# Three re-placements in a step table of an attention and feed-forward kernel: pair 1's projections, the norm products of the steps without a tail, and the tail's second up products

## The reference

```python
q = einsum('bsd,hde->bhse', x, Wq); k, v alike
scores = where(causal, q @ k.T / sqrt(64), -inf)
out = softmax(scores) @ v
y = x + heads @ Wo;  y = layernorm(y, 1e-3) * gamma + beta
x1 = layernorm(x + y, 1e-5)
h = silu(x1 @ wg.T) * (x1 @ wu.T)          # int weights / 127
out = layernorm(x1 + h @ wd.T, 1e-5)
```

## Time and profile before

| what | value |
|---|---|
| median of 3 runs | 1460.8 us (1460.03 to 1463.27) |
| the profiled execution's own time | 1462.12 us |
| its span in the profile | 1459.7 us |
| mean granted TensorE clock | 0.991 of 2.4 GHz |
| PE, DVE, ACT, POOL busy | 96%, 69%, 69%, 69% |
| instructions in the trace | 23745 |

### The profile page before, as it was taken

One profiled execution on the slowest core, in us unless ns is written; L12 is line 12 of the kernel. 1 busy time (PEld: TensorE's weight loads), 2 busy tenths in 40 slices (PEclk: granted clock), 3 DMA queues, 4 the chain that ended last, 5 costly groups with the idle time before them and its releaser, 6 DMA issues.

```text
span 1459.7 us, 23745 instructions
## 1 busy us (share of the span) xinstructions
PE 1403.6 (96%) x7936; PEld 1227.6 (84%) x7936; DVE 1014.0 (69%) x2729; ACT 1003.8 (69%) x1924; POOL 1003.9 (69%) x944
## 2 busy tenths in 40 slices
PE   6999999999999999999999999999999999999876
PEld 5788888888888888888888888888888888888766
DVE  7766666766666676776667676776766667677874
ACT  4776777767676676766668676686867668676534
POOL 4676766666686775868668586785868668587744
PEclk9999999999999999999999999999999999999988
DMA  4333222312342221321232122132223223122000
GB/s 135 97 81 96 64 60 95 116 52 68 108 131 72 61 88 53 90 85 44 88 116 95 52 59 68 59 117 55 78 66 102 88 59 95 52 59 59 23 11 30
DMA packets 61241, 110.45 MB, mean 76 GB/s; under 512 B 16256, under 2 KB 41600, under 8 KB 61120
## 3 DMA queue, kind: packets, MB, share of 16 engines
q1 hardware_dynamic: 61120, 108.94, 25.0%
HBM read 60.95 MB, written 13.89 MB: 51 GB/s over the span
## 4 chain that ended last, share of the span: by engine, by line
PE 81%; DVE 9%; POOL 4%; ACT 3%; issue 2%; DMA 1%; ACTq 0%; SPq 0%; POOLq 0%
PE bank L787 24%; PE bank L760 16%; PE bank L660 12%; PE bank L736 9%; PE bank L723 7%; PE bank L685 5%; PE bank L822 5%; PE bank L834 3%; POOL probs_lo L1403 2%; DVE K L1121 1%; DVE max_part L1156 1%; POOL h_lo L1445 1%; DVE bank L1154 1%; ACT probs_hi L972 1%; ACT probs L969 1%
## 5 line engine op out<-in xcount | busy, mean ns | idle before, releaser
L1403 POOL TENSOR_TENSOR probs_lo<-probs,probs_hi 128x512 fp32r<-128x512 f32 x576 | 744.1, 1299 | 401.0 <-ACT probs_hi L972 397.8
L969 ACT ACTIVATE probs<-bank 128x512 f32<-128x512 f32 x576 | 344.4, 598 | 304.4 <-DVE bank L1170 219.5
L760 PE MATMUL bank<-Q,K 128*128 128x512 f32 (+3 forms) x1536 | 385.3, 352 | 5.2 <-ACT probs_hi L972 4.5
L972 ACT ACTIVATE probs_hi<-bank 128x512 fp32r<-128x512 f32 x576 | 342.6, 595 | 0.0
L760 PEld LDWEIGHTS bank<-Q,K 128*128 128x128 f32 x1536 | 252.8, 190 | 33.6 <-ACT probs_hi L972 5.7
L736 PE MATMUL bank<-K,Q 128*128 128x512 f32 (+3 forms) x768 | 245.6, 362 | 8.4 <-DVE max_part L1154 6.3
L1154 DVE CUSTOM_DVE_ANT_0 bank<-bank,mask_keys_free 128x128 f32<-128x128 f32 (+3 forms) x512 | 243.3, 506 | 3.4 <-PE bank L736 3.0
L787 PE MATMUL bank<-probs_hi,VH 128*128 128x512 f32 (+3 forms) x768 | 232.0, 343 | 6.0 <-POOL probs_lo L1403 5.3
L787 PE MATMUL bank<-probs_lo,VH 128*128 128x512 f32 (+3 forms) x768 | 234.6, 346 | 0.0
L787 PE MATMUL bank<-probs_hi,VL 128*128 128x512 f32 (+3 forms) x768 | 234.4, 346 | 0.0
L1170 DVE TENSOR_TENSOR bank<-bank,mask_queries_free 128x256 f32<-128x256 f32 (+1 forms) x320 | 119.6, 374 | 148.1 <-PE bank L760 147.0
(11 more groups left out here) (170 smaller groups left out, 2224.3 us busy)
## 6 DMA issues: line engine op xcount, KB each, us to landing
Q<-Q SPq DMA_DIRECT2D x64, 256.0 KB, 3.7
K<-K SPq DMA_DIRECT2D x64, 256.0 KB, 3.4
recip_bc<-recip_scratch SPq DMA_DIRECT2D x62, 256.0 KB, 3.4
wh<-w_scratch SPq DMA_DIRECT2D x12, 768.0 KB, 4.9
wl<-w_scratch SPq DMA_DIRECT2D x12, 768.0 KB, 6.6
wo_quad<-wo SPq DMA_DIRECT2D x16, 256.0 KB, 3.2
y<-x SPq DMA_DIRECT2D x16, 256.0 KB, 3.4
x_tail<-x SPq DMA_DIRECT2D x13, 256.0 KB, 3.1
```

What stands on the lines that cost most here:

```text
L760: last = mm(bk[:, at:at + cols], KX[:, n, P * i:P * i + P], QX[:, n, q0:q0 + cols], start=(KX is K1 and at == 0), stop=(KX is K2 and at + ...
L969: A(pe_[:, g % 2, :], stb[g % 2][:, :], ACT.Exp).then_inc(exp_done, 1)
L972: A(ph[:, g % RING, :], stb[g % 2][:, :], ACT.Exp).then_inc(hi_done, 1)
L1403: G.tensor_tensor(pl[:, g % RING, :], pe_[:, g % 2, :], ph[:, g % RING, :].bitcast(F32), ALU.subtract).then_inc(lo_done, 1)
```

## The change

It does three things. `P1_AT` becomes [-1, 0, 1, 2]: the units 1, 2 and 3 of pair 1 are issued one step earlier in groups 1 to 15 (the first group has its own table). The second block of up products of the steady tails (groups 5 to 14) moves from step 23 to step 22, and with it tanh and GLU from 24 to 23 and `h_lo` from 25 to 24; its down products stay in step 26. And the norm products are issued by DVE, behind the maximum and the projections' low parts of the step, while no tail runs (groups 0 to 4), and by POOL as before afterwards: 18 of 62 move. They keep their steps.

```diff
-P1_AT, P1_AT_FIRST = [-1, 1, 2, 3], [-5, -4, -3, -2]
+P1_AT, P1_AT_FIRST = [-1, 0, 1, 2], [-5, -4, -3, -2]
...
-STEADY = tail_at(-5, -1, 7, [9, 23, 29], [13, 26, 32], 36)
+STEADY = tail_at(-5, -1, 7, [9, 22, 29], [13, 26, 32], 36)
...
+        def norms(g):
+
+            for half in range(2):
+                for r in range(2):
+                    i, rest = divmod(g - NS * (2 * r + 1) - NORM_AT[r][half], NST)
+                    if rest == 0 and 0 <= i < NIT - 1:
+                        yield 2 * i + r, half
+                if g == NG - NST + NS + NORM_AT_LAST[half]:
+                    yield 2 * (NIT - 1), half
...
+            def norm(pair, half):
+
+                cols = slice(CH * half, CH * half + CH)
+                if half == 0:
+                    dve.wait_ge(recip_bc, 16 * (2 * pair + 2))
+                V.tensor_tensor(HT[:, pair % 3, cols], HT[:, pair % 3, cols], RB[:, cols], ALU.mult).then_inc(ht_norm, 1)
...
+                if not running(it):
+                    for pair, half in norms(g):
+                        norm(pair, half)
                 h, k = divmod(g - (C1_DONE + LAG + 2), NS)
                 if k == 0 and 0 <= h < NH - 2:
                     recip(h)
...
-                for half in range(2):
-                    for r in range(2):
-                        i, rest = divmod(g - NS * (2 * r + 1) - NORM_AT[r][half], NST)
-                        if rest == 0 and 0 <= i < NIT - 1:
-                            norm(2 * i + r, half)
-                    if g == NG - NST + NS + NORM_AT_LAST[half]:
-                        norm(2 * (NIT - 1), half)
+                if running(it):
+                    for pair, half in norms(g):
+                        norm(pair, half)
```

## The result

The changed kernel took 1464.4 us (median of 16 runs, 1463.24 to 1466.78), the kernel before, beside it on the same chip, 1461.82 us (16 runs, 1459.18 to 1464.11). The ratio is **1.0019**, with a 95% interval of 1.0012 to 1.0026: 2.6 us by the medians, 2.8 by the ratio, where the sum of the prediction had +1.1. Against the 0.2% that the prediction sets as its bound it is "no change", at the upper edge, but the interval does not hold 1.

The account below looks back on a forecast made before the run. PE's own work was taken as the bound (busy 96% of the span), so only its waits could change. -4.0 - 0.5 + 5.6 = +1.1 us on the median 1460.8 gave 1461.9 us, range 1452 to 1468.

Parts of the forecast that it names:

- the 0.2% that the prediction sets as its bound: Whole kernel: times within 0.2% of the median, 2.9 us, can't be told from no change; chance of that 0.40.
- The forecast's case: Whole kernel: all three estimates hold, +1.1 us to 1461.9 us, own range 1458.5 to 1465; chance 0.50.
- Norm products, -4.0: Step 12, groups 1 to 4: PE's wait for POOL's probs_lo mostly goes; -4.0 us, bounds -4.6 and -2.5.
- the rival by which the move does nothing: Step 12 keeps half or all its wait, DVE's product and probs_lo excluding one another longer; +3 to +5 us, chance 0.10.
- Pair 1, -0.5: Groups 5 to 15: step 6 loses a 0.76 us wait, step 4 gets 0.74; -0.5 us, bounds -8.4 and +7.7.
- The allowance for group 5: Group 5, step 4: no OUT ahead, so ACT starts some 0.3 us earlier.
- ACT's backlog decides: Step 4, eleven groups: PE waits 1.5 us instead of 0.74; sum +9.5 us, 1470.3 us, chance 0.12.
- Up products, +5.6: Steps 24 to 26, ten groups: 1.05 us later, 0.49 of waiting removed, 0.56 each; +5.6 us, bounds -4.9 and +10.5.
- The early up block is free: Steps 22 to 26: step 26's wait goes and no new one comes; -4.9 for this edit, 1451.4 us, chance 0.12.
- Groups 6 to 14: These nine groups together: from 786.4 us, 9 x 0.54 more, 791 us; prediction wrong if shorter than 786.

Follow-up runs that it names:

- the control: Kernel before with only N1 (ACT) and the gamma product (POOL) a step later, pair 1 not moved: 1460.78 against 1461.81 us, ratio 0.9993.
- the repairs: Second up block in step 22, norm products on DVE, h_lo in step 25, t_glu behind the maximum: 0.9992; plus early pair 1, late N1: 0.9968; plus later GLU products: 0.9952.

## Why the prediction was right, and where it was off

**The forecast's case held.** All three edits did what the working said, in the steps it named. The time is above its 1461.9 by 2.5 us, inside the forecast's own range of 1458.5 to 1465. It is not right by errors that cancel: by the ratios of the single edits each of the three terms came out somewhat worse than its estimate, -3.2 for -4.0, -0.1 for -0.5, +6.1 for +5.6. Part of that isn't the change: the kernel before took 1461.82 in the comparison, a microsecond over the 1460.8 that the sum started from. Sum against measurement is +1.1 against +2.6 to +2.8.

**Norm products, -4.0.** Right in size: groups 1 to 4 are 3.9 us shorter in the full change; with this edit alone they are 2.7 shorter in the trace, where group 3 had the late transfer, and the ratio gives 3.2 (1.9 to 4.5). PE's product with V of step 10 starts 0.16 us late in group 2, priced at 0 to 0.2, and step 12 keeps 0.25. The one bound that failed is that of the product on DVE: not 0.62 to 1.49 us but 0.71 to 1.72. By the rows it is no length of its own, but 0.55 us and what is left of POOL's instruction. It cost nothing on DVE, as the 0.79 us of room and the 2.90 us of step 12 behind it were enough. (The lower bound of the gain should read -2.4 and not -2.5: 4.6 less four waits of 0.55.) So the rival by which the move does nothing fell: POOL had to be rid of 1.29 us, and the product beside it adds some 0.46 to one probs_lo (1.75 against 1.29). The lock between the two engines that the Trainium skill's page "SBUF — State Buffer", section "SBUF: two separate sides", states agrees with the trace: all 18 products end 0.55 us behind the POOL instruction that was running, and the probs_lo started during a product ends 1.14 to 1.18 behind it.

**Pair 1, -0.5.** The mechanism was right, down to the queue: the control and the run with N1 behind the exponentials show that step 4 waits for what stands ahead on ACT. The gain of step 6 was right (0.76 predicted, 0.78 measured), the loss of step 4 was sized too small: 0.74 predicted, 0.86 measured, of which 0.78 is the late start that the working reckoned and 0.08 the slower products behind the wait. The allowance for group 5 (ACT 0.3 us earlier, so 0.44) was also too good: it took 0.68. Together -0.5 became between -0.1 (the ratio of this edit alone) and +0.7 (0.08 in ten groups, -0.13 in group 5). The rival "ACT's backlog decides" had the right place, but its price of 1.5 us a group was not reached.

**Up products, +5.6.** Right: +0.56 a group predicted, +0.64 measured (step 24 +0.59, step 26 +0.05), which is 6.4 us in ten groups, and 6.1 by the ratio. The parts agree as well: 1.05 us later for the product with V of step 24 predicted, and 0.58 + 0.44 = 1.02 measured; 0.49 removed, and 0.49 measured where nothing took its place. I had "some 0.6" of the 1.05 in step 24, for the maximum, and that is what the row shows. "The early up block is free" is excluded by the run with `h_lo` in step 25, and each of the repairs says which instruction stood in the way.

**Groups 6 to 14** were predicted at 791 us and took 791.89. Against the kernel before, freed of its single wait, they grew by some 6.5 us and not by 4.9; nine times the 0.12 us of step 4 and the 0.08 of steps 24 and 26, less the 0.02 more that step 6 gained, 1.6 us, make the difference. **What failed in kind** were the expectations behind it, which followed a queue only as far as the next wait: step 25 behind the GLU was not foreseen, step 27 behind `h_lo` only in part and as the rival, and step 5 behind gamma and step 7 behind the statistics were priced too low.

## What to carry to other kernels

In a pipeline whose engines walk through the same steps in a fixed order, a wait is a property of a queue: before moving something, write down for each queue it leaves and enters what stands ahead of the next instruction that PE waits for, and go on until nothing is late. A long step covers late work of others, so a block is not only its own wait; moving the down products from step 26 to 27 made the two steps 0.69 us longer. And putting an instruction behind its neighbours on its engine (`t_glu`, `h_lo`, and N1 once pair 1 was early) gained here, where moving work between steps mostly exchanged waits.

## What the runs showed that was not expected

**A two-operand product on DVE can take 1.72 us** beside POOL, 0.714 at the least, for 128 x 512 float32; the range taken from the four instructions on `xl` was too narrow. Both engines' instructions get longer in turn, each when it is the one that starts second: 0.55 us behind the other's end for DVE, 1.14 to 1.18 for POOL.

**The clock falls at places that differ from run to run.** PE stands idle for 2.4 us near the start of group 0 in both kernels. The timeline of the kernel before, then, in a fence of its own, that of the changed one:

```profile
42.01 0.79 PE L760 MATMUL bank<-Q,K 128*128 128x384 f32 x4 [2.39 <-ACT probs_hi L972]
...
44.09 0.63 PE L787 MATMUL bank<-probs_lo,VH 128*128 128x512 f32 x1
```

```profile
43.03 0.79 PE L770 MATMUL bank<-Q,K 128*128 128x384 f32 x4 [2.38 <-ACT probs_hi L982]
...
44.85 0.39 PE L797 MATMUL bank<-probs_lo,VH 128*128 128x512 f32 x1
```

After the same idle time the first kernel's matmuls take 0.63 us where the other's take 0.39. The window of the kernel before at that place shows half of the full clock, 1.2 GHz of 2.4:

```profile
43.00:46.40 3.40, 2.95 (x8) 2.34 (x8) 0.93 (x3) 1.38 (x3) 2.86 (x3) 0.50 0.00 0
```

In the changed kernel the like falls into the last group, in a window from 1374 on whose clock is 0.68; the eight down products there take 2.08 us:

```profile
1374.00:1378.00 4.00, 4.00 (x17) 3.52 (x17) 1.79 (x7) 1.87 (x4) 2.98 (x6) 0.68 0.00 0
```

This is what made group 0 shorter by 1.4 and group 15 longer by 1.0 us in one trace each. In both traces it begins behind an idle PE, of 2.39 us here and of 1.50 us there, and at the ends of the program. A pair of single executions can therefore differ by one or two microseconds at the ends for nothing that a change did; the steps in the middle, where the clock is 1.00, mostly repeat to some 0.1 us. The exceptions in these traces are step 12 of group 3, where ACT waits for a transfer (4.01 to 4.47 us without the norm edit), step 26 of groups 3 and 4 (2.16 to 3.04 and 1.56 to 2.53) and now and then step 8 of a group with a tail (once 2.63 for 1.64).
